# The second bias of a first MLP: a one-row pass on TensorE, or an addition on VectorE

## The reference

```
h2 = layernorm(x, n2_w, n2_b)
mlp = gelu(h2 @ lin1_w + lin1_b) @ lin2_w + lin2_b
x = x + mlp
```

## Time and profile before

| | us |
|---|---|
| median of 3 runs | 886.29 |
| lowest and highest | 885.42, 890.17 |
| the profiled execution | 886.6 |
| its span, first to last instruction | 884.9 |
| TensorE busy | 822.8 (93%) |
| VectorE busy | 455.8 (52%) |
| ScalarE busy | 469.1 (53%) |
| GpSimd busy | 185.7 (21%) |

### The profile page before, as it was taken

How to read it: one execution, slowest core, us unless ns; L and a number is a source line. 1 busy time by engine, 2 the same in 40 slices (tenths; PEclk the granted TensorE clock), 3 DMA queues, 4 the chain that set the end, 5 groups by cost and what they waited for, 6 DMA issues and landing times.

```text
span 884.9 us, 14666 instructions
## 1 busy us (share of the span) xinstructions
PE 822.8 (93%) x5272; PEld 664.9 (75%) x5272; DVE 455.8 (52%) x1005; ACT 469.1 (53%) x961; POOL 185.7 (21%) x257
## 2 busy tenths in 40 slices
PE   1989989979979899998998999999999999999998
PEld 0866766766676578887887678985999679986988
DVE  4888688697787824446663640056102740155001
ACT  5977578568568633336553734445233733455232
POOL 3050041023010022226500450026000450025000
PEclk9999999999999979999998999999999999999999
DMA  7010000000000010001100300000000000000000
GB/s 209 1 29 14 1 19 21 0 11 24 0 1 1 2 39 12 12 13 37 50 1 1 126 1 1 1 18 0 0 0 0 18 0 0 0 18 1 1 1 19
DMA packets 12710, 15.48 MB, mean 17 GB/s; under 512 B 5312, under 2 KB 10560, under 8 KB 12544
## 3 DMA queue, kind: packets, MB, share of 16 engines
q1 hardware_dynamic: 10656, 9.46, 3.5%
q0 software_dynamic: 2016, 5.51, 2.2%
HBM read 13.39 MB, written 1.57 MB: 17 GB/s over the span
## 4 chain that ended last, share of the span: by engine, by line
PE 76%; DVE 10%; ACT 7%; issue 4%; DMA 1%; SPq 1%; POOL 0%; DVEq 0%; ACTq 0%; POOLq 0%
PE ps L222 19%; PE ps L1599 14%; PE ps L1514 6%; PE ps L1241 5%; PE ps L1614 5%; PE ps L1159 4%; PE ps L1333 4%; PE ps L1139 3%; DVE area L284 2%; ACT area L1061 2%; ACT area L946 2%; PE ps L1147 2%; PE ps L1119 1%; PE ps L1539 1%; PE ps L1199 1%
## 5 line engine op out<-in xcount | busy, mean ns | idle before, releaser
L1599 PE MATMUL ps<-area 128*128 128x192 f32 x768 | 127.4, 326 | 0.0
L222 PE MATMUL ps<-xs,ws 128*128 128x512 f32 x460 | 122.1, 416 | 5.7 <-DVE xs L511 3.7
L1599 PEld LDWEIGHTS ps<-area 128*128 128x128 f32 x768 | 124.8, 190 | 2.1 <-issue 0.5
L222 PE MATMUL ps<-ws,wx 128*128 128x512 f32 x480 | 116.1, 397 | 1.3 <-DVE ws L827 1.3
L1087 ACT ACTIVATE area<-ps,bcol 128x512 f32<-128x512 f32 x96 | 65.7, 688 | 86.7 <-PE ps L222 86.7
L838 DVE TENSOR_TENSOR area<-ps,area 128x384 f32<-128x384 f32 x32 | 17.9, 558 | 177.9 <-PE ps L1599 177.8
L222 PEld LDWEIGHTS ps<-xs,ws 128*128 128x128 f32 x460 | 88.0, 197 | 26.0 <-issue 6.6
L222 PEld LDWEIGHTS ps<-ws,wx 128*128 128x128 f32 x480 | 89.2, 188 | 22.7 <-DVE ws L827 3.0
L946 ACT ACTIVATE area<-ps,nm 112x196 f32<-112x196 f32 (+1 forms) x240 | 85.6, 441 | 19.8 <-DVE nm L646 19.8
L423 POOL TENSOR_TENSOR area<-area,dstat 128x512 f32<-128x512 f32 x32 | 38.0, 1197 | 251.5 <-DVE dstat L781 251.5
L646 DVE TENSOR_REDUCE nm<-ps 112x4 f32<-112x784 f32 (+1 forms) x72 | 62.6, 873 | 26.3 <-PE ps L1139 21.3
(11 more groups left out here) (177 smaller groups left out, 1353.4 us busy)
## 6 DMA issues: line engine op xcount, KB each, us to landing
stage<-in_wall POOLq DMA_DIRECT2D x42, 128.0 KB, 2.4
area<-in_w2e SPq DMA_DIRECT2D x1, 2304.0 KB, 8.3
out<-xres SPq DMA_DIRECT2D x4, 384.0 KB, 2.6
xres<-in_x SPq DMA_DIRECT2D x1, 1152.0 KB, 6.8
area<-in_wall SPq DMA_DIRECT2D x2, 512.0 KB, 6.3
area<-in_w2a SPq DMA_DIRECT2D x1, 576.0 KB, 3.8
room<-in_rel SPq DMA_DIRECT2D x4, 128.0 KB, 5.6
xres<-in_x SPq DMA_DIRECT2D x1, 384.0 KB, 3.1
```

What stands on the lines that cost most here:

```text
L222: last = mm(out_, l, r, start=n == 0, stop=n == len(pairs) - 1)
L1599: last = mm(ps[:, 4 + b, s * D:s * D + D], hTd[:, m, b * T + s * P:b * T + s * P + P], w2x[:, e * MC + m, :], start=m == 0, stop=m == MC - 1)
```

## The change

The one-row matmul at the head of each output tile is taken out, and the first of the six matmuls starts the PSUM chain instead. The bias row goes into the array `bias_rows`, which now has three rows; the first load of `brow` takes rows 0 and 1 of it. When the windowed attention is over and `w2l` has been asked for, SyncE fetches the third row into row 0 of `brow`, which nobody reads any more. In `body_b` VectorE waits for that row (`ld_b`) and adds it to the pair's four tiles of `xres` in one instruction, after the norm of the next pair and ahead of the split; ahead of the residual it waits for that addition (`b_bias`).

```diff
@@ SyncE
-            for dst, src in (..., (brow[:], bias_rows), ...
+            for dst, src in (..., (brow[:], bias_rows[:, 0:2, :]), ...
...
             sp.wait_ge(o_res, 1 + 2 * PAIRS)
             sp.dma_start(w2l, w2a).then_inc(ld_l2, 16)
+            sp.dma_start(brow[:, 0, :], bias_rows[:, 2, :]).then_inc(ld_b, 16)
@@ VectorE
             def body_b(it, nxt):
                 front_norm(it + (PAIRS + 1), it + 1 if nxt else 0, NT)
+
+                dve.wait_ge(ld_b, 16)
+                rows = xres[:, bass.ds(it * NT, NT), :]
+                V.tensor_tensor(rows, rows, brow[:, 0, :].unsqueeze(1).broadcast_to([P, NT, D]), ALU.add).then_inc(b_bias, 1)
                 front_split(it + (PAIRS + 1), NT, (b_h, MC * it + MC))
+                dve.wait_ge(b_bias, it + 1)
                 residual(it, (4, 5), b_y, it, b_res)
@@ TensorE
                 for j in range(NT):
                     dst = ps[:, 4 + j // 2, (j % 2) * D:(j % 2) * D + D]
-
-                    mm(dst, ot1[L2ROW:L2ROW + 1, 0:P], wproj[L2ROW:L2ROW + 1, 0, 1, :], start=True, stop=False)
                     for m in range(MC):
                         if j == 0 and m == MC - 1:
                             pe.wait_ge(b_gelu, 1 + it * MC + MC)
-                        last = mm(dst, hT[:, m, j * P:j * P + P], w2l[:, m, :], start=False, stop=m == MC - 1)
+                        last = mm(dst, hT[:, m, j * P:j * P + P], w2l[:, m, :], start=m == 0, stop=m == MC - 1)
```

More of the change, by code:

```diff
@@ L62 @@
 A_CHUNKS = CW1 // CHUNK
-L2ROW = 96
 VB = 7 * HD
@@ L193, in build @@
             sem(n) for n in ("o_tr", "o_td", "o_ta", "o_proj", "o_res"))
-        b_h, b_gelu, b_y, b_res = (
-            sem(n) for n in ("b_h", "b_gelu", "b_y", "b_res"))
+        b_h, b_gelu, b_y, b_res, b_bias, ld_b = (
+            sem(n) for n in ("b_h", "b_gelu", "b_y", "b_res", "b_bias", "ld_b"))
         c_qk, c_v, c_qt, c_ve, c_s, c_nm, c_p, c_t, c_pt, c_o = (
@@ L295, in _ @@
                 sp.dma_start(first[:, k], wall[:, 0:QKV]).then_inc(ld_q, 16)
-            for dst, src in ((ident[:], c_ident), (bcol[:], bias_cols), (brow[:], bias_rows), (kc, c_keys),
+            for dst, src in ((ident[:], c_ident), (bcol[:], bias_cols), (brow[:], bias_rows[:, 0:2, :]), (kc, c_keys),
                              (kec, c_border), (pt[:, 0, 0, 0:P], c_mask)):
@@ L1658, in lay_out @@
         wp[:, n, 0], wp[0:R1, n, 1], wp[R1, n, 1] = w[0:P], w[P:], b
-    wp[L2ROW, 0, 1] = v["c_lin2_b"]
     cols = np.zeros((P, 48), f)
@@ L1671, in lay_out @@
     cols[:, E1B:E1B + NE * MC] = v["f_b1"].reshape(NE * MC, P).T
-    rows = np.concatenate([cb[None, 2 * D:], ab[None, 2 * D:], v["f_b2"]])
+    rows = np.concatenate([cb[None, 2 * D:], ab[None, 2 * D:], v["c_lin2_b"][None], v["f_b2"]])
     def key(y, xx, y0=0, y1=0, x0=0, x1=0):
@@ L1696, in lay_out @@
         w2e=v["f_w2"].reshape(NE * MC, P, D).transpose(1, 0, 2), bias_cols=cols,
-        bias_rows=np.broadcast_to(rows[None, 0:2], (P, 2, D)), b2r=np.broadcast_to(rows[None, 2:], (P, NE, D)),
+        bias_rows=np.broadcast_to(rows[None, 0:3], (P, 3, D)), b2r=np.broadcast_to(rows[None, 3:], (P, NE, D)),
         c_ident=np.eye(P, dtype=f),
```

## The result

The changed kernel takes 875.61 us (median of 4 runs, 874.08 to 876.62), the kernel before 885.86 us beside it (4 runs): a ratio of 0.9869, with a 95% interval of 0.9848 to 0.9889. That is about 10.3 us less, where 11.3 were forecast (875.0 us). Later runs beside the experiments gave 0.9876 (0.9847 to 0.9905) and 0.9886 (0.9850 to 0.9923).

What follows compares the result with a forecast made beforehand. The prediction took TensorE, busy 93% of the span with 76% of the chain, as the bound. 886.6 us less 11.3 for the passes is 875.3, and 0.3 lower for the median gives 875.0; 8-in-10 range 872.0 to 880.0.

Steps and rivals of the forecast that it cites:

- The pass that goes: First MLP on TensorE: removing 16 one-row passes and the loader's stops saves 11.3 us, bounds 10.3 to 11.9.
- second parts: TensorE's transposes and four output tiles in each first-MLP pair; four together forecast to fall from 45.75 to 34.5 us.
- rival of 881.1 us: Only the passes go, the loader's stops in the first MLP stay: gain 5.2 us; chance 6%.
- What is late next: First MLP, TensorE's next products: VectorE's split is still in time, by 0.39 us, so nothing is lost.
- rival of the late split: The split becomes the bound behind the second transpose: up to 5.5 us turns into waiting, down to 880.5; chance 8%.
- The addition: VectorE, one add per pair between normalised rows and split: 0.95 us each, hidden in idle time, no cost on the path.
- The sum: Whole kernel: 886.6 - 11.3 = 875.3 us for the profiled execution; the median, 0.3 lower, gives 875.0.
- The row: SyncE's extra 96 KB fetch lands at about 320 us, needed by 329.5, costing nothing; rival that it is late: 3%.
- The clock: Rival: the half-speed stretch of about 6 us near 480 us goes (872.0) or comes twice (878.0); chance 13%.

Runs made afterwards that it cites:

- 128-row experiment: Changed kernel with the bias again a TensorE pass heading each output tile, but of 128 rows, and no VectorE addition: 882.52 us, ratio 0.9943.
- grouped passes: Kernel before with its one-row passes two by two (tile order 0, 2, 1, 3), no VectorE addition: 883.76 us, ratio 0.9959.
- late fetch: Changed kernel with the row's fetch held back until the first two output tiles of the first pair are done: 877.33 us.

## Why the prediction was right

*The pass that goes.* The forecast was 11.3 us off TensorE's path; the four second parts lost 11.4, and the span at an equal clock 11.1 (0.3 either way). That the median of four runs came within 0.6 us of the 875.0 forecast is in part luck, as the clock shows below. The step that decided was to price the passes by starts, not by their count: two passes for each of 16 tiles are 5.2 us, and the 128-row experiment measured just that. The rest, 6.2 us, is the weight loader's stops at the one-row passes, 6.7 us in the list of waits. The grouped passes, half the changes at the same count, gave back 3.1 us and halved the stops. So the rival of 881.1 us fell, and of the two rules of the Trainium skill it is that of "TensorEngine Tiling (Array Packing)", section Key Properties (a change of tiling mode drains TensorE), that the trace agrees with. No row names the tiling mode, so that this is the reason is not shown. The loads themselves do take about as long with one row as with 128, 0.18 and 0.19 us each in the trace of the kernel before; what failed is only the step from there to a one-row pass at the price of a plain one.

*What is late next.* Forecast: 4.25 us from the second transpose to the products, the split ready at 3.86, so 0.39 us to spare. Measured: 351.92 - 347.71 = 4.21, and the split ends 0.46 us earlier, 0.34 with the hand-over taken off. The rival of the late split fell.

*The addition.* 0.95 us was forecast from two shapes that were not its own, and 0.94 to 0.95 measured. That it is hidden was shown from two sides: without it nothing is gained in the span, and behind the split it costs 2.0 us of the stage.

*Around the span.* The sum kept the 1.7 us beside the span as they were; the changed kernel has 2.1. The forecast thus put 0.4 us at nothing, and the gain in the time at an equal clock is 10.7 us (0.3 either way). The addition and the fetch, with their semaphores, bring it, since without them it is 1.70. How they do is not shown: with the fetch but no addition (the 128-row experiment, which also fills a tile and adds two waits on TensorE) it is 1.94.

*The row.* Forecast to land 4.5 us after its issue with room up to 329.5 us; it took 3.6 us, and the late fetch showed that beyond the cover the time is lost to TensorE's wait.

*The clock.* This was the weak step: I gave a stretch at half clock, won or lost, 13%, at one place, and read a single execution's clock as the kernel's own. Every profile holds several such stretches, and their length changes from one execution to the next; in the first profile the one near 480 us was not gone but half as long, and another stood near 50 us. The runs of the kernel before spread over some 9 us, nearly all of it along the line over the clock. The difference of the kernels does not hang on that, but a single execution does. The first medians, of four runs each, stood 10.3 apart and not 11.1; 0.4 us of that is the time outside the span, and the clock is the likely reason for the rest.

## What to carry to other kernels

Price a pass on TensorE by the starts around it and not by its duration or count: a pass with one row among passes with 128 cost more than twice a plain one, and a bias in a full tile, or passes of one row kept together, would have saved part of that without any other engine. Work moved to another engine costs nothing on the path where that engine waits anyway, so look for the wait and not for the busy share. And before a difference of a microsecond is read from medians, look at what else varies between the runs: here the stage's own rows and the granted clock told differences of 1 to 2 us that the medians hid.

## What the runs showed of the hardware

The stop of some 0.2 us comes with a change between the one-row pass and 128 rows, but not between 65 and 128. In the causal attention's projection of the changed kernel, passes of 128 and of 65 rows take turns:

```profile
462.38 0.49 PE L1423 MATMUL ps<-wproj,area 128*128 128x192 f32 x2
462.71 0.49 PE L1424 MATMUL ps<-wproj,area 65*128 65x192 f32 x2
463.04 0.49 PE L1423 MATMUL ps<-wproj,area 128*128 128x192 f32 x2
```

Each pair of passes starts 0.33 us after the last, as plain ones do. The same trace has passes of 64 rows (L1373) behind ones of 128 in twelve places, and the loader stops ahead of them only where TensorE waits for ScalarE. Ahead of the 128-row passes that follow there (L1377) it stops 4.0 us in twelve times, but the type changes with the rows, to bf16. Two things are not separated: the one row also lies on another partition, 96, where the 65 rows begin at 0. And which numbers of rows between 1 and 64 bring the stop was not tried.
